# One pass of the attention scores made for two slots at once, on quarters of TensorE's rows

## The chip, the cores and the metric

The kernel runs on one core of a Trainium2 chip. The metric is the time of one execution on the device, in microseconds (us). The unchanged kernel takes 734.6 us, the median of three runs.

## The reference

A block on x of shape (2, 1024, 128): causal attention with a residual, a mixture of experts, a state space layer, and the mixture again. Only the attention is touched. Cut to what matters:

```
qk = layernorm(x) @ W_qk;  q, k = split(qk)          # 16 heads of 64, two batches of 1024 tokens
scores = einsum('bhid,bhjd->bhij', q * 64**-0.5, k)  # masked above the diagonal
out = einsum('bhij,bhjd->bhid', softmax(scores), k)  # the keys are also the values
x = x + out @ W_out
```

## The kernel before

**Units.** The attention works in 16 units: a pair of heads in one of the two batches. A head of the pair has 64 rows, so head l = 0 lies on partitions 0 to 63 and head l = 1 on partitions 64 to 127. Most products of the attention are made for both heads by two matmuls, one on each half of TensorE's rows (the profile writes such a tile 64*128, rows by columns).

**Slots.** The masked scores of a unit are laid out transposed (keys on partitions, queries along the free axis) in nine slots of 512 columns for each head, with one or two segments in a slot (`SLOTS`). Slots 0 and 3 to 7 are one segment of 512 columns, slot 1 is 384 + 128, slot 2 is 256 + 256, slot 8 is 384 + 128. `scores(unit, slot)` makes four passes over each segment, for both heads in each: high keys by high queries (L753), high by low (L756), low by high (L759), and a pass that subtracts each query's maximum (L762). In that last pass the stationary operand is all ones, and the moving operand `m_rows` holds the negated maxima: eight rows of each head's 64 are used, one for each tile of 128 queries, picked by `neg_pick`; all other rows are zero. For diagonal slots (0, 1, 2, 7, 8) `mask` adds the mask first (L738).

**The maxima** of unit u+1 are found one unit ahead: `max_scores` (ten fills "M", L716) makes plain scores on TensorE, `maxima` on VectorE (L583, L587) reduces them into `half_max`, and `join_maxima` (L596) joins the halves into `row_max`. `turn_max` transposes that (L726), and `max_rows` (L601) spreads it into `m_rows`.

**The order** is written out by hand. Each unit after the first goes through five rounds:

```
ROUNDS = [[("mask", 0), ("M", 0), ("S", 0), ("M", 1)],
          [("mask", 1), ("mask", 2), ("M", 2), ("S", 1), ("S", 2), ("M", 3)],
          [("M", 4), ("S", 3), ("S", 4), ("M", 5)], [("M", 6), ("S", 5), ("S", 6), ("M", 7)],
          [("mask", 7), ("mask", 8), ("M", 8), ("S", 7), ("S", 8), ("M", 9)]]
```

At the start of a round TensorE makes `outputs` of the previous unit (probabilities by keys, L783, tile 128*64), and in rounds 1 and 3 `denominators` (L802, tile 128*32). After round 4 it projects the keys "K" and queries "Q" of the unit after next (L680 to L682, tile 128*128). Unit 0 has an order of its own, `FIRST_ROUNDS`, in which S and M alternate. Unit 15 has no M, and units 14 and 15 project nothing.

**The ring.** Every T (transposed keys), M, S, K and Q takes the next of three pairs of PSUM banks, in strict rotation (`ring_uses`). `pair_free` makes TensorE wait until the use three places earlier has been read. So M 4 takes the banks of S 1, S 3 those of S 2, M 6 those of S 3, S 5 those of S 4, S 7 those of S 6, K those of S 7, and Q those of S 8. A slot's banks come free when ScalarE has taken its exponentials (L525, one instruction of 1024 columns for each slot, slots in order).

**Other engines.** GpSimd adds up the probabilities for the denominators (`add_up`, L427), eleven sums to a unit, the first of which needs slot 1. VectorE also makes the low parts and scales the outputs. SyncE loads weights and spreads the inverted denominators.

Of the kernel before, what the change touches and what calls it, by code (L numbers as in the profile page):

```python
# [20 lines left out]
ALU = mybir.AluOpType  # L21
# [3 lines left out]
P = 128  # L25
# [212 lines left out]
def attention(nc, k, w_qk, x_view, load_w_out):  # L238
# [5 lines left out]
    with Scope(nc, "at") as s:  # L244
# [31 lines left out]
        knat_ps_ready, knat_done = s.sem("knat_ps_ready"), s.sem("knat_done")  # L276
        max_ready, max_taken, row_max_done = s.sem("max_ready"), s.sem("max_taken"), s.sem("row_max_done")
        rows_ps_ready, rows_done = s.sem("rows_ps_ready"), s.sem("rows_done")
        scores_ready, exp_done, av_done, summed = s.sem("scores_ready"), s.sem("exp_done"), s.sem("av_done"), s.sem("summed_up")
        den_ready, ln_done, inv_done, out_used = s.sem("den_ready"), s.sem("ln_done"), s.sem("inv_done"), s.sem("out_used")  # L280
        inv_spread = [s.sem(f"inv_spread{h}") for h in range(2)]

# [2 lines left out]
        def rows(l):  # L285

            return slice(DH * l, DH * l + DH)

        def dens(g, halves):

# [51 lines left out]
        def split_w(pool, p):  # L342
            pool.wait_ge(w_loaded, 16 * (p + 1))
            wait(pool, proj_ready, 4 * (p - 1))
            pool.tensor_copy(w_hi[p % 2][:, :, :], w_raw[:, :, :]).then_inc(w_split, 1)
            pool.wait_ge(w_split, 2 * p + 1)
            pool.tensor_tensor(w_lo[p % 2][:, :, :], w_raw[:, :, :], w_hi[p % 2][:, :, :].bitcast(FP32),
                               ALU.subtract).then_inc(w_split, 1)

        def set_up(pool):  # L350
            pool.memset(k.eps[:, :], EPS).then_inc(k.ident_made, 1)
            pool.memset(k.ident[:, :], 0.0).then_inc(k.ident_made, 1)
            pool.wait_ge(k.ident_made, 2)
            pool.affine_select(out=k.ident[:, :], in_=k.ident[:, :], compare_op=ALU.not_equal, fill=1.0,
                               base=0, pattern=[[-1, P]], channel_multiplier=1).then_inc(k.ident_made, 1)
            pool.memset(eye2[:, :, :], 0.0).then_inc(consts, 1)
            pool.memset(mask2[:, :, :], 0.0).then_inc(consts, 1)
            pool.memset(neg_pick[:, :], 0.0).then_inc(consts, 1)
            pool.memset(after_query[:, :], 0.0).then_inc(consts, 1)
            pool.wait_ge(consts, 4)  # L360
            pool.affine_select(out=after_query[:, BANK - P:BANK], in_=after_query[:, BANK - P:BANK], compare_op=ALU.is_ge,
                               fill=MASKED, base=0, pattern=[[-1, P]], channel_multiplier=1).then_inc(consts, 1)
            pool.wait_ge(consts, 5)
            for l in range(2):
                pool.affine_select(out=eye2[rows(l), :, :], in_=eye2[rows(l), :, :], compare_op=ALU.not_equal, fill=1.0,
                                   base=0, pattern=[[DH, 2], [-1, P]], channel_multiplier=1).then_inc(consts, 1)
                pool.affine_select(out=mask2[rows(l), :, :], in_=mask2[rows(l), :, :], compare_op=ALU.is_ge, fill=MASKED,
                                   base=0, pattern=[[DH, 2], [-1, P]], channel_multiplier=1).then_inc(consts, 1)
                pool.affine_select(out=neg_pick[rows(l), :], in_=neg_pick[rows(l), :], compare_op=ALU.not_equal, fill=-1.0,
                                   base=0, pattern=[[-1, QT]], channel_multiplier=1).then_inc(consts, 1)  # L370
            pool.wait_ge(consts, 11)
            split_w(pool, 0)

        def clear(dve):
# [9 lines left out]
        with nc.Block() as block:  # L384
# [83 lines left out]
            def _(act):  # L468
# [49 lines left out]
                    act.activation(to, to, ACT.Exp, scale=-1.0).then_inc(inv_done, 1)  # L518

                def exponentials(unit, slot):  # L520
                    act.wait_ge(scores_ready, 2 * (NSLOT * unit + slot) + 2)
                    if unit:
                        act.wait_ge(av_done, 2 * (NBURST * (unit - 1) + BURST_OF[slot]) + 2)
                        act.wait_ge(summed, NSUM * (unit - 1) + SUMMED_AT[slot] + 1)
                    act.activation(probs[:, :, slot * BANK:(slot + 1) * BANK], pair("S", unit, slot)[:, :, :], ACT.Exp,  # L525
                                   scale=BETA).then_inc(exp_done, 1)
# [41 lines left out]
            def _(dve):  # L568
# [24 lines left out]
                def join_maxima(unit):  # L593
                    dve.wait_ge(max_taken, NMAX * (unit + 1))
                    wait(dve, rows_ps_ready, 2 * unit)
                    dve.reduce_max(row_max[:, :, 0:QT], half_max[:, :, :, :], AX.X).then_inc(row_max_done, 1)  # L596

                def max_rows(unit):

# [38 lines left out]
                for m in range(6, NMAX):  # L638
                    maxima(0, m)
                join_maxima(0)  # L640
                dve.wait_ge(consts, 11)
                for unit in range(UNITS):
                    more = unit + 1 < UNITS
                    for r, row in rounds(unit):
# [24 lines left out]
            def _(pe):  # L669
# [50 lines left out]

                def turn_max(unit):

                    pe.wait_ge(row_max_done, unit + 1)
                    wait(pe, ln_done, 2 * unit - 1)
                    for l in range(2):
                        pe.matmul(misc[rows(l), 0:P], row_max[:, l, :], k.ident[:, :], start=True, stop=True)\  # L726
                          .then_inc(rows_ps_ready, 1)
# [13 lines left out]
                def scores(unit, slot):  # L741

                    u, out, first = unit % 2, pair("S", unit, slot), slot not in DIAGONAL
                    if slot == 0:
                        pe.wait_ge(rows_done, unit + 1)
                        pe.wait_ge(k_low, unit + 1)
                        pe.wait_ge(q_low, unit + 1)
                    pair_free(pe, "S", unit, slot)
                    for seg, (j, a, b) in enumerate(SLOTS[slot]):
                        q, keys, o = slice(a * P, b * P), slice(j * P, (j + 1) * P), at_slot(slot, seg) - slot * BANK  # L750
                        to = [out[:, l, o:o + (b - a) * P] for l in range(2)]
                        for l in range(2):
                            pe.matmul(to[l], kh[u][rows(l), keys], qh[u][rows(l), q], start=first, stop=False,  # L753
                                      skip_group_check=True)
                        for l in range(2):
                            pe.matmul(to[l], kh[u][rows(l), keys], ql[u][rows(l), q], start=False, stop=False,  # L756
                                      skip_group_check=True)
                        for l in range(2):
                            pe.matmul(to[l], kl[u][rows(l), keys], qh[u][rows(l), q], start=False, stop=False,  # L759
                                      skip_group_check=True)  # L760
                        for l in range(2):
                            last = pe.matmul(to[l], ones_r[rows(l), :], m_rows[u][rows(l), q], start=False, stop=True,  # L762
                                             skip_group_check=True)
                            if seg + 1 == len(SLOTS[slot]):
                                last.then_inc(scores_ready, 1)

                def outputs(g, r):

# [67 lines left out]
                turn_keys(1)  # L836
                turn_max(0)
                warm(5, out_ps)
                pe.wait_ge(consts, 11)

                for unit in range(UNITS + 1):
                    more = unit + 1 < UNITS
                    for r, row in rounds(unit):
                        if r == 0 and 0 < unit < UNITS:
                            turn_max(unit)
                        if unit:
                            outputs(unit - 1, r)
                        if r == (1 if unit < UNITS else 3) and unit:
                            denominators(unit - 1, 1)
                        if unit == UNITS:  # L850
                            continue
                        if r == (3 if unit else 4):
                            denominators(unit, 0)
                        if r == 0 and unit and more:
                            turn_keys(unit + 1)
                        for what, n in row:
                            if what == "mask":
                                mask(unit, n)
                            elif what == "S":
                                if n in DIAGONAL and not unit:  # L860
                                    mask(unit, n)
                                scores(unit, n)
                            elif more:
                                max_scores(unit + 1, n)
                        if r == NBURST - 1 and unit + 2 < UNITS:
                            project(unit + 2, "K")
                            project(unit + 2, "Q")
# [1023 lines left out]
```

## Time and profile before

| | |
|---|---|
| median of 3 runs | 734.6 us (734.4 to 735.08) |
| the profiled execution | 734.34 us |
| its span in the profile | 732.5 us |
| TensorE busy | 706.9 us (96%) |
| VectorE, ScalarE, GpSimd busy | 434.5, 371.4, 417.4 us |
| granted TensorE clock over the span | 0.993 |

The attention fills the stretch up to about 452 us, the rest is the two mixtures and the state space layer. In the profile PE is TensorE's matmuls, PEld its weight loads, DVE VectorE, ACT ScalarE, POOL GpSimd. Matmul records overlap, since the array is pipelined: what a pass costs is the distance from its start to the next start, not the duration printed beside it.

### The profile page before, as it was taken

How to read it: one execution, taken by the hardware profiler on the slowest of the kernel's cores; microseconds unless marked ns; L12 is line 12 of the kernel's file. 1: busy time of each engine (PE TensorE's matmuls, PEld its weight loads, DVE VectorE, ACT ScalarE, POOL GpSimd, SP SyncE). 2: the span in 40 equal slices, each digit the busy share in tenths (PEclk: the TensorE clock that was granted, in tenths of full speed). 3: DMA queues.
4: the chain of work that ended last, by engine and by line, in shares of the span. 5: the costliest groups of instructions: out<-in, count | busy, mean ns of one | idle time of the engine just before them, and what ended most of it. 6: DMA issues, size and time to landing. Idle time of an engine off the chain costs nothing. (4 is left out here: it accounts for less than half of the span.)

```text
span 732.5 us, 14992 instructions
## 1 busy us (share of the span) xinstructions
PE 706.9 (96%) x5681; PEld 498.8 (68%) x5681; DVE 434.5 (59%) x1214; ACT 371.4 (51%) x478; POOL 417.4 (57%) x310
## 2 busy tenths in 40 slices
PE   7999999999999999999999899999999999889998
PEld 5665666566665566566656555978888865678887
DVE  7776765765676676676567600635654656755433
ACT  4465655555555555465555442364664343566421
POOL 4486677668559659658756864144544421254543
PEclk9799999999999999999999999999999999999999
DMA  2001001001001100100100112623323000043332
GB/s 72 8 17 26 24 19 30 24 16 30 24 18 28 30 16 22 36 17 17 30 16 16 30 44 63 153 89 103 98 79 102 1 0 1 12 134 103 105 103 72
DMA packets 41276, 33.49 MB, mean 46 GB/s; under 512 B 14002, under 2 KB 32756, under 8 KB 41204
## 3 DMA queue, kind: packets, MB, share of 16 engines
q1 hardware_dynamic: 41204, 32.52, 15.5%
q8 instruction: 46, 0.75, 0.4%
q14 instruction: 26, 0.21, 0.1%
HBM read 23.32 MB, written 1.31 MB: 34 GB/s over the span
## 5 line engine op out<-in xcount | busy, mean ns | idle before, releaser
L427 POOL TENSOR_TENSOR all_x<-all_x,at_probs 128x1024 f32<-128x1024 f32 (+3 forms) x128 | 208.2, 1627 | 19.0 <-ACT at_probs L525 0.4
L525 ACT ACTIVATE at_probs<-at_ring 128x1024 f32<-128x1024 f32 x144 | 144.3, 1026 | 100.6 <-PE at_ring L762 99.4
L587 DVE CUSTOM_DVE_ANT_0 at_ring<-at_ring,at_after_query 128x128 f32<-128x128 f32 (+3 forms) x252 | 116.9, 516 | 68.9 <-PE at_ring L716 68.9
L783 PE MATMUL at_both<-at_probs,at_k_nat 128*64 128x512 f32 (+1 forms) x736 | 134.3, 493 | 0.2 <-issue 0.2
L1279 POOL TENSOR_TENSOR m_prod<-m_gate,m_wb 128x512 f32<-128x512 f32 x64 | 81.5, 1281 | 91.0 <-ACT m_gate L1141 81.8
L427 POOL TENSOR_TENSOR all_x<-at_probs 128x768 f32<-128x768 f32 (+1 forms) x32 | 67.3, 2104 | 106.6 <-ACT at_probs L525 103.9
L583 DVE TENSOR_REDUCE at_half_max<-at_ring 128x2 f32<-128x1024 f32 x64 | 78.4, 1226 | 44.9 <-PE at_ring L716 44.9
L783 PEld LDWEIGHTS at_both<-at_probs,at_k_nat 128*64 128x64 f32 x736 | 47.0, 136 | 65.3 <-issue 54.3
L1195 DVE TENSOR_TENSOR m_hid<-m_prod,m_u 128x512 f32<-128x512 f32 x64 | 43.6, 686 | 75.7 <-POOL m_prod L1279 69.3
L1057 PEld LDWEIGHTS m_acc<-rest_wd,m_hid 128*128 128x128 f32 (+1 forms) x576 | 74.4, 191 | 7.9 <-DVE m_hid L1195 2.2
L1057 PE MATMUL m_acc<-rest_wd,m_hid 128*128 128x128 f32 (+1 forms) x576 | 76.1, 276 | 0.0
L1141 ACT ACTIVATE m_gate<-m_g 128x512 f32<-128x512 f32 (+1 forms) x72 | 42.6, 597 | 64.2 <-PE m_g L1048 63.0
L716 PE MATMUL at_ring<-at_kh,at_qh 64*128 64x512 f32 (+2 forms) x380 | 70.8, 396 | 1.0 <-ACT a_room L478 0.5
L759 PE MATMUL at_ring<-at_qh,at_kl 64*128 64x512 f32 (+3 forms) x384 | 67.1, 343 | 0.0
L753 PE MATMUL at_ring<-at_qh,at_kh 64*128 64x512 f32 (+3 forms) x384 | 67.0, 344 | 0.1
L762 PE MATMUL at_ring<-at_m_rows,at_ones_r 64*128 64x512 f32 (+3 forms) x384 | 66.9, 342 | 0.0
L756 PE MATMUL at_ring<-at_ql,at_kh 64*128 64x512 f32 (+3 forms) x384 | 66.8, 342 | 0.0
L716 PEld LDWEIGHTS at_ring<-at_kh,at_qh 64*128 64x128 f32 x380 | 34.6, 187 | 27.0 <-issue 25.5
L753 PEld LDWEIGHTS at_ring<-at_qh,at_kh 64*128 64x128 f32 x384 | 36.7, 185 | 4.6 <-ACT at_probs L525 0.8
L759 PEld LDWEIGHTS at_ring<-at_qh,at_kl 64*128 64x128 f32 x384 | 36.6, 185 | 4.0
L762 PEld LDWEIGHTS at_ring<-at_m_rows,at_ones_r 64*128 64x128 f32 x384 | 36.7, 185 | 3.8
L756 PEld LDWEIGHTS at_ring<-at_ql,at_kh 64*128 64x128 f32 x384 | 36.5, 185 | 3.8
(256 smaller groups left out, 1194.6 us busy)
## 6 DMA issues: line engine op xcount, KB each, us to landing
m_wb<-m_wt_far SPq DMA_DIRECT2D x128, 128.0 KB, 2.9
at_inv<-at_inv_q SPq DMA_DIRECT2D x240, 32.0 KB, 1.9
all_x<-in_L_attn_a_x SPq DMA_DIRECT2D x8, 256.0 KB, 4.2
at_w_raw<-in_L_attn_a_W_qk SPq DMA_DIRECT2D x8, 128.0 KB, 2.6
out<-all_x SPq DMA_DIRECT2D x4, 256.0 KB, 2.3
a_room<-in_L_attn_a_W_out SPq DMA_DIRECT2D x1, 512.0 KB, 4.1
m_raw_wg<-in_L_ffn_experts_wg SPq DMA_DIRECT2D x1, 512.0 KB, 3.8
m_raw_wu<-in_L_ffn_experts_wu SPq DMA_DIRECT2D x1, 512.0 KB, 3.9
```

Source lines behind the costliest of these rows:

```text
L427: return pool.tensor_tensor(sums[:, :, a * P:b * P], left, right, ALU.add)
L525: act.activation(probs[:, :, slot * BANK:(slot + 1) * BANK], pair("S", unit, slot)[:, :, :], ACT.Exp, scale=BETA).then_inc(exp_done, 1)
L583: last = dve.reduce_max(half_max[:, :, i, out], pair("M", unit, m)[:, :, at:at + w], AX.X)
L587: last = dve.tensor_tensor_reduce(out=sums_ps, in0=sums_ps, in1=after_query[:, BANK - w:BANK], scale=1.0, scalar=MASKED, op0=ALU.add, op1= ...
L716: last = pe.matmul(out[:, l, at:at + (b - a) * P], qh[u][rows(l), i * P:(i + 1) * P], kh[u][rows(l), a * P:b * P], start=True, stop=True)
L753: pe.matmul(to[l], kh[u][rows(l), keys], qh[u][rows(l), q], start=first, stop=False, skip_group_check=True)
L756: pe.matmul(to[l], kh[u][rows(l), keys], ql[u][rows(l), q], start=False, stop=False, skip_group_check=True)
L759: pe.matmul(to[l], kl[u][rows(l), keys], qh[u][rows(l), q], start=False, stop=False, skip_group_check=True)
L762: last = pe.matmul(to[l], ones_r[rows(l), :], m_rows[u][rows(l), q], start=False, stop=True, skip_group_check=True)
L783: last = pe.matmul(out_bank(g, int(r > 0))[rows(l), o:o + (b - a) * P], k_nat[g % 3][:, j, rows(l)], probs[:, l, at:at + (b - a) * P], sta ...
L1057: last = pe.matmul(acc[:, t * P:(t + 1) * P], hid[g % BUFS][h, t * P:(t + 1) * P], f.wd[h, st, :], start=(st == 0 and t == 0), stop=(st == ...
L1279: pool.tensor_tensor(prod[g % BUFS][:, :], gate[g % BUFS][:, :], wb[q % SPREAD][:, :], ALU.mult)\
```

## The change

The last of the four passes is taken out of `scores` and put into a function of its own, `shift(unit, slots)`. In units 1 to 15 it is called once in a round, behind the last S of the round, for all slots of the round (one in round 0, two in rounds 1 to 4). In unit 0 it is called behind each slot. It uses 32 rows for a matmul in place of 64: the first slot of a call takes rows 0 to 31 (head 0) and 64 to 95 (head 1), the second rows 32 to 63 and 96 to 127. For that, `join_maxima` writes the maxima twice, 32 columns apart, and `neg_pick` gets its diagonal twice, by two more instructions of GpSimd in the set-up. ScalarE now waits on one of two semaphores, for even and for odd slots. `turn_max` waits for both reductions.

```
+        def quarter_rows(l, n):
+            return slice(DH * l + DH // 2 * n, DH * l + DH // 2 * (n + 1))
...
             pool.wait_ge(consts, 11)
+            for l in range(2):
+                pool.affine_select(out=neg_pick[rows(l), :], in_=neg_pick[rows(l), :], compare_op=ALU.not_equal, fill=-1.0,
+                                   base=-DH // 2, pattern=[[-1, QT]], channel_multiplier=1).then_inc(consts, 1)
+            pool.wait_ge(consts, 13)
             split_w(pool, 0)
...
                 def exponentials(unit, slot):
-                    act.wait_ge(scores_ready, 2 * (NSLOT * unit + slot) + 2)
+                    of = (NSLOT + 1 - slot % 2) // 2
+                    act.wait_ge(shifted[slot % 2], 2 * (of * unit + slot // 2) + 2)
...
                     dve.reduce_max(row_max[:, :, 0:QT], half_max[:, :, :, :], AX.X).then_inc(row_max_done, 1)
+                    dve.reduce_max(row_max[:, :, DH // 2:DH // 2 + QT], half_max[:, :, :, :], AX.X).then_inc(row_max_done, 1)
...
-                    pe.wait_ge(row_max_done, unit + 1)
+                    pe.wait_ge(row_max_done, 2 * unit + 2)
...
-                        for l in range(2):
-                            last = pe.matmul(to[l], ones_r[rows(l), :], m_rows[u][rows(l), q], start=False, stop=True,
-                                             skip_group_check=True)
-                            if seg + 1 == len(SLOTS[slot]):
-                                last.then_inc(scores_ready, 1)
+
+                def shift(unit, slots):
+                    u = unit % 2
+                    for seg in range(2):
+                        for n, slot in enumerate(slots):
+                            if seg >= len(SLOTS[slot]):
+                                continue
+                            j, a, b = SLOTS[slot][seg]
+                            o = at_slot(slot, seg) - slot * BANK
+                            for l in range(2):
+                                r = quarter_rows(l, n)
+                                last = pe.matmul(pair("S", unit, slot)[:, l, o:o + (b - a) * P], ones_r[r, :],
+                                                 m_rows[u][r, a * P:b * P], start=False, stop=True, skip_group_check=True)
+                                if seg + 1 == len(SLOTS[slot]):
+                                    last.then_inc(shifted[slot % 2], 1)
...
                                 scores(unit, n)
+                                if not unit:
+                                    shift(unit, [n])
+                                elif n == slots[-1]:
+                                    shift(unit, slots)
```

## Rows read from the trace of the kernel before

**Rows 1.** The page's busy time: us, share of the span, instructions.

```profile
PE 706.9 (96%) x5681; PEld 498.8 (68%) x5681; DVE 434.5 (59%) x1214; ACT 371.4 (51%) x478; POOL 417.4 (57%) x310
```

**Rows 2.** Windows: unit 11, from one L726 to the next; stretch, length, busy us.

```profile
315.18:341.58 26.40, 26.40 (x250) 16.66 (x249) 17.53 (x42) 14.56 (x19) 17.61 (x11) 1.00 0.09 22
```

**Rows 3.** Timeline of PE, rounds 1 to 3 of unit 11: start, us, instruction, operands.

```profile
322.88 0.34 PE L753 MATMUL at_ring<-at_qh,at_kh 64*128 64x384 f32 x2
...
324.86 0.28 PE L762 MATMUL at_ring<-at_m_rows,at_ones_r 64*128 64x256 f32 x2
324.98 0.34 PE L716 MATMUL at_ring<-at_kh,at_qh 64*128 64x384 f32 x2
325.24 1.08 PE L783 MATMUL at_both<-at_probs,at_k_nat 128*64 128x512 f32 x4
326.25 0.50 PE L716 MATMUL at_ring<-at_kh,at_qh 64*128 64x512 f32 x2
326.59 0.40 PE L753 MATMUL at_ring<-at_qh,at_kh 64*128 64x512 f32 x2
...
333.68 1.94 PE L783 MATMUL at_both<-at_probs,at_k_nat 128*64 128x512 f32 x12
```

**Rows 4.** Timeline of PE, round 4 of unit 11, slots 7 and 8, and K.

```profile
336.19 0.39 PE L753 MATMUL at_ring<-at_qh,at_kh 64*128 64x512 f32 x2
...
336.88 0.40 PE L762 MATMUL at_ring<-at_m_rows,at_ones_r 64*128 64x512 f32 x2
337.12 0.34 PE L753 MATMUL at_ring<-at_qh,at_kh 64*128 64x384 f32 x2
...
337.64 0.34 PE L762 MATMUL at_ring<-at_m_rows,at_ones_r 64*128 64x384 f32 x2
337.81 0.22 PE L753 MATMUL at_ring<-at_qh,at_kh 64*128 64x128 f32 x2
...
338.10 0.27 PE L762 MATMUL at_ring<-at_m_rows,at_ones_r 64*128 64x128 f32 x2
338.21 0.44 PE L716 MATMUL at_ring<-at_kh,at_qh 64*128 64x512 f32 x2
338.58 0.50 PE L680 MATMUL at_ring<-all_xhi,at_w_hi 128*128 128x512 f32 x1
338.92 0.39 PE L681 MATMUL at_ring<-all_xlo,at_w_hi 128*128 128x512 f32 x1
```

**Rows 5.** Timeline of ACT: exponentials of slots 7, 8 (unit 10) and 1, 2 (unit 11).

```profile
310.95 2.12 ACT L525 ACTIVATE at_probs<-at_ring 128x1024 f32<-128x1024 f32 x2 [2.73 <-PE at_ring L762]
...
324.21 2.02 ACT L525 ACTIVATE at_probs<-at_ring 128x1024 f32<-128x1024 f32 x2 [1.03 <-PE at_ring L762]
```

**Rows 6.** Timeline of POOL and PE, unit 11: the sums, then the denominators.

```profile
327.81 2.16 POOL L427 TENSOR_TENSOR all_x<-all_x,at_probs 128x256 f32<-128x256 f32 x2
...
330.60 0.64 PE L802 MATMUL at_both<-all_x,at_ones 128*32 128x256 f32 x8
```

**Rows 7.** Timeline: the end of POOL's set-up, and DVE's joining.

```profile
4.80 0.20 POOL L369 TENSOR_SCALAR_AFFINE_SELECT at_neg_pick<-at_neg_pick 64x8 f32<-64x8 f32 x1
6.11 0.40 POOL L345 CAST at_w_hi<-at_w_raw 128x256 fp32r<-128x256 f32 x1 [1.11 <-DMA at_w_raw<-in_L_attn_a_W_qk]
...
313.76 0.19 DVE L596 TENSOR_REDUCE at_row_max<-at_half_max 128x16 f32<-128x32 f32 x1
```

**Rows 8.** Timeline of ACT and PE, ends of units 0 and 14.

```profile
47.17 1.02 ACT L525 ACTIVATE at_probs<-at_ring 128x1024 f32<-128x1024 f32 x1 [0.60 <-PE at_ring L762]
...
48.34 0.47 PE L680 MATMUL at_ring<-all_xhi,at_w_hi 128*128 128x512 f32 x1 [0.69 <-ACT at_probs L525]
...
419.58 0.44 PE L726 MATMUL at_both<-all_ident,at_row_max 128*64 128x128 f32 x4 [1.75 <-DVE at_row_max L596]
```

**Rows 9.** Timeline of POOL and PE, last unit: first sum, last denominators.

```profile
428.69 1.82 POOL L427 TENSOR_TENSOR all_x<-at_probs 128x768 f32<-128x768 f32 x1 [5.20 <-ACT at_probs L525]
...
447.73 1.08 PE L797 MATMUL at_both<-all_x,at_ones 128*64 128x512 f32 x4 [0.63 <-POOL all_x L427]
```

More of the change, by code:

```diff
@@ L278, in attention @@
         rows_ps_ready, rows_done = s.sem("rows_ps_ready"), s.sem("rows_done")
-        scores_ready, exp_done, av_done, summed = s.sem("scores_ready"), s.sem("exp_done"), s.sem("av_done"), s.sem("summed_up")
+        shifted = [s.sem("shifted_even"), s.sem("shifted_odd")]
+        exp_done, av_done, summed = s.sem("exp_done"), s.sem("av_done"), s.sem("summed_up")
         den_ready, ln_done, inv_done, out_used = s.sem("den_ready"), s.sem("ln_done"), s.sem("inv_done"), s.sem("out_used")
@@ L640, in _ @@
                 join_maxima(0)
-                dve.wait_ge(consts, 11)
+                dve.wait_ge(consts, 13)
                 for unit in range(UNITS):
@@ L838, in _ @@
                 warm(5, out_ps)
-                pe.wait_ge(consts, 11)
+                pe.wait_ge(consts, 13)
                 for unit in range(UNITS + 1):
@@ L855, in _ @@
                             turn_keys(unit + 1)
+                        slots = [n for what, n in row if what == "S"]
                         for what, n in row:
```

## The prediction

> **What bounds the kernel now.** I read the page first: TensorE is busy for 96% of the span, no other engine over 60% [rows 1]. A share says little, so next the windows of single units. From one L726 to the next a unit takes 26.40 us with PE busy for all 26.40, while ACT has 14.56, DVE 17.53 and POOL 17.61 [rows 2]. So for units 1 to 13 each us that TensorE saves or spends inside a unit shows in the end, unless something then makes it wait. Third the timeline of TensorE inside that unit. The reader is to look at distances between starts. A pass of 512 columns for both heads moves the next start by 0.24 (336.88 to 337.12), one of 384 by 0.17, one of 128 by 0.11 [rows 4], one of 256 by 0.12 [rows 3]. Last ACT's timeline, since a slot's banks are held until its exponential is done [rows 5]. ACT is idle half of the time, but what counts is when its work ends against the ring.
>
> **The saving.** L762's passes now cost, in round 1 (slots 1 and 2), 0.17 + 0.11 + 0.12 + 0.12 = 0.52 us; in rounds 2 and 3 two passes of 512, 0.46; in round 4, 0.24 + 0.17 + 0.11 = 0.52 [rows 3, 4]. With two slots side by side the wider segment of each pair counts: round 1 0.17 + 0.12 = 0.29, rounds 2 and 3 0.23 each, round 4 0.24 + 0.11 = 0.35. Saved: 0.23 + 0.23 + 0.23 + 0.17 = 0.86 us a unit. Round 0 has one slot and saves nothing. That four tiles run together I take from the denominators: eight matmuls of 256 columns on quarters of the columns take 0.64 us in all [rows 6], far below eight in a row. No row has quarters of the rows.
>
> On four tiles of 32 rows the Trainium skill (TensorE: Matmul & The Clock Gate, "Measured speedup vs the span model") gives a measured speed-up of 3.07 for 512 columns, not 4. By that, as an estimate, a pass of four would take 0.24 x 4 / 3.07 = 0.31 in place of 0.24, and the sum below would be some 3 us higher; no row here shows it.
>
> **The switches.** The trace does not show a change from tiles of 64 rows to tiles of 32. It shows every other change of tile, and none is free. From 64*128 to 128*128: the pass of 512 columns at 338.21 is followed after 0.37, not 0.24, and the first one in the new tile after 0.34 (338.58 to 338.92) [rows 4]; so 0.13 before and 0.10 after. From 64*128 to 128*64 a pass of 384 takes 0.26 in place of 0.17, 0.09 more; back at 64*128 the first pass of 512 takes 0.34, 0.10 to 0.11 more [rows 3]. I read these as the array running empty, and then a weight load with nothing to hide behind. One switch is thus 0.20 to 0.24 us. The `shift` passes lie between scores and M, both on 64*128, so each round gets two more switches, 0.41 us with the lower figures. Bounds: 0 below (if a change among divisions of rows is not a change at all), 0.46 above. I take 0.41, since all kinds that are shown pay, among them the one in which only the number of rows differs.
>
> The Trainium skill (TensorEngine Tiling (Array Packing), "Key Properties") states that changing the tiling mode, not just the tile, drains the engine, and counts 64 and 32 rows as different modes. The rows agree for every change that they hold. By that rule rounds 0 to 4 spend 2.05 us on switches to save 0.86; without it the saving stands alone.
>
> **The exponentials come later.** Before, ACT could begin on the first slot of a round while TensorE made the second. Now both slots are ready at the end, and two exponentials of 1.02 stand in a row behind them [rows 5]. Two uses of the ring stand close behind.
>
> *Round 1, S 3 waits for slot 2's banks.* Before: exponentials from 324.21 to 326.23 [rows 5], S 3 at 326.59 [rows 3], 0.36 to spare. Now: slots 1 and 2 start at 322.88 and M 3 follows at 324.98; less 0.52 the three other passes end at 324.46. Running empty 0.09 and load 0.11: 324.66. The second pass of four starts 0.17 later and lands 0.28 after its start: 325.11. ACT follows 0.07 later (slot 7's pass 336.88 + 0.40 = 337.28, its exponential one unit of 26.40 before at 310.95 [rows 4, 5]): 325.18. Two exponentials, 2.02: 327.20. From ACT's end to TensorE's start 0.15 (47.17 + 1.02 = 48.19 to 48.34 [rows 8]): S 3 at 327.35, against 326.59 + 0.18 by TensorE's own work (0.41 - 0.23). So a wait of 0.58, and round 1 costs 0.76.
>
> *Round 4, K waits for slot 7's banks.* Before: K at 338.58 [rows 4], slot 7's exponential done some 0.2 earlier. Now: the other passes end at 338.21 - 0.52 = 337.69, + 0.20 switch + 0.40 for the pass + 0.07 + 1.02 + 0.15 = K at 339.53. That is 0.95 late, of which TensorE's own work is 0.41 - 0.17 = 0.24 and 0.71 is a wait. Behind K in TensorE's queue stand Q, the next unit's L726 and outputs, all late by the same; ACT's and DVE's copies of K and Q follow K as before. Q needs slot 8, done about 1 us after slot 7, when K's 1.4 us of passes are still running: no wait.
>
> *Rounds 2 and 3.* The same lateness meets 1.94 us of outputs before the next use [rows 3]: no wait with the switches, 0.41 - 0.23 = +0.18 each. *Round 0*: +0.41, no wait.
>
> Sum for a unit of 1 to 13: 0.41 + 0.76 + 0.18 + 0.18 + 0.95 = 2.48 us, times 13 = 32.2 us.
>
> **The other units.** Unit 0 has nine calls with one slot each: nothing saved, nine times 0.41 = 3.7. It has waits that take some up, but its K stands behind slot 8's exponential already [rows 8], so most goes through: 3.4, bounds 0 and 9 x 0.46 = 4.1. Unit 14 projects nothing and ends on DVE (1.75 us of idle TensorE before L726 [rows 8]): what counts is when M 9 starts, 337.69 + 0.20 + 0.24 + 0.11 + 0.09 = 338.33, 0.12 late in round 4. 0.41 + 0.76 + 0.18 + 0.18 + 0.12 = 1.65, plus the second joining, 0.19 at most [rows 7]: 1.8. Unit 15 ends on GpSimd: its sums run almost without a gap from 428.69 until the last denominators, which wait 0.63 for them [rows 9], and the first of them needs slot 1. Slot 1's exponential comes 0.97 late as in round 1, plus 0.2 from round 0's switch (no M follows there, so one switch more, not two): 1.2.
>
> **What I cost at nothing.** The two instructions in GpSimd's set-up, 0.20 each [rows 7], lie under a wait of 1.11 us for weights; without it, 0.4. The second joining in units 1 to 13 lies under K and Q: the first begins at 313.76 [rows 7] and L726, which waits for it, at 315.18 [rows 2], 1.2 after its end. In unit 0 it does not: 0.2. Queued behind it on DVE is the scaling of outputs, which nobody waits for at once. The sums on GpSimd start 0.97 later; the two that the denominators need end at 329.97, now 330.94, while TensorE comes to them at 330.60 + 0.76 + 0.18 = 331.54 [rows 6]. No DMA changes.
>
> Sum: 32.2 + 3.4 + 1.8 + 1.2 + 0.2 = 38.8 us. The profiled execution took 734.34 (span 732.5), 0.26 below the median. 734.3 + 38.8 = 773.1; I forecast 772. With 0.46 for two switches all rounds but the waits' share grow by 0.05 each, some 3 us; with 0 it is rival A.
>
> **The rivals.**
>
> *A, free switches, late exponentials.* For it: no row has this change of tile. Against: all others pay. Round 0 gives 0. Round 1: 324.46 + 0.17 + 0.28 + 0.07 + 2.02 + 0.15 = 327.15, +0.56. Round 2 -0.23. Round 3 -0.13, as S 7's mask would now wait 0.1 for slot 6. Round 4: 337.69 + 0.40 + 0.07 + 1.02 + 0.15 = 339.33, +0.75. 0.95 x 13 = 12.4, units 14 and 15 1.0, joining 0.2: 748. The mode rule above is what stands against it. Switches that cost half lie between, at 760.
>
> *B, the quarters do not run side by side*, so the change does not do what it says: slots' passes one behind the other. The 0.86 are not saved in 14 units, and the last landing is later still by up to 0.2: 772 + 12 = 784. Against: a pair on two halves of the rows takes 0.24, hardly more than one matmul of 512 columns would alone at 2.4 GHz, and quarters of columns overlap [rows 4, 6].
>
> *C, faster.* Its place is the ring: if the exponentials' lateness were hidden at S 3 and at K, and the switches free, 0.86 x 14 = 12 us come off: 722. It decides where slot 2 is done before TensorE gets to S 3, that is 0.8 us earlier than my sum has it. Against: ACT needs 2.02 for the pair, and between the shift and S 3 stand only M 3, 1.0 of outputs and M 4 [rows 3]. I see no way round.
>
> **How the numbers follow.** Full switches: 62%, its own range 763 (waits a third shorter than worked out) to 780 (the upper bound of the switches and of unit 0, and passes of four slower than pairs). A and half-price switches: 23%, 746 to 762. B: 8%, 781 to 790. C: 5%. No change (waits and saving cancel): 2%. The range takes in the first two and stops at 746 and 781, which leaves out C, most of B and no change. Within 0.2% (1.5 us) is what a measurement can't tell from no change: faster 0.05, same 0.02, slower 0.93.
>
> **What would show it.** In the changed kernel L762's successor should stand in tiles 32*128, with a gap of 0.1 before it and 0.34 for its first pass of 512. A unit should take 28.9 us. TensorE should be idle twice a unit: before L753 of slot 3 (0.6) and before L680 (0.7), both put down to L525. ACT's pairs should start 1 us later in the round. Were the passes 0.24 apart with no gap, A is right; four starts in two steps of 0.23 would be B. The prediction is wrong above all if the switch within divisions of rows costs other than 0.2.

## The result, and the profile after

The changed kernel takes 767.4 us (median of 4 runs, 767.0 to 767.66) against 734.64 for the kernel before: a ratio of 1.0446, 95% interval 1.0434 to 1.0458. It is slower by 32.8 us. The forecast was 772, within 746 to 781. The four executions spread by 0.66 us, so the noise doesn't matter to the sign or the size.

The page of the changed kernel: its span and the busy time of the engines.

```profile
span 765.4 us, 15012 instructions
...
PE 724.0 (95%) x5681; PEld 488.9 (64%) x5681; DVE 436.3 (57%) x1230; ACT 368.3 (48%) x478; POOL 417.0 (54%) x312
```

TensorE is busy for 17 us more than in [rows 1], with the same number of matmuls, and for 16 us more it is not busy. Both halves of the prediction are in these two numbers, but which is which the page can't say: a matmul whose weights are still being loaded counts as busy. So, windows of one unit, the changed kernel's unit 11, as in [rows 2]:

```profile
337.96:366.42 28.46, 27.42 (x250) 15.96 (x249) 17.69 (x43) 14.32 (x19) 17.32 (x12) 1.00 0.08 20
```

28.46 us in place of 26.40, of which TensorE is busy 27.42. Units 1 to 13 have 28.41 to 28.52. Now the same unit's timeline of PE, round 0 and then rounds 1 and 2; it answers to [rows 3].

```profile
341.94 0.42 PE L770 MATMUL at_ring<-at_qh,at_kl 64*128 64x512 f32 x2
342.30 0.50 PE L784 MATMUL at_ring<-at_m_rows,at_ones_r 32*128 32x512 f32 x2
342.73 0.50 PE L727 MATMUL at_ring<-at_kh,at_qh 64*128 64x512 f32 x2
343.16 1.51 PE L805 MATMUL at_both<-at_probs,at_k_nat 128*64 128x512 f32 x8
...
347.37 0.28 PE L770 MATMUL at_ring<-at_qh,at_kl 64*128 64x256 f32 x2
347.58 0.51 PE L784 MATMUL at_ring<-at_m_rows,at_ones_r 32*128 32x384 f32 x8
348.02 0.44 PE L727 MATMUL at_ring<-at_kh,at_qh 64*128 64x384 f32 x2
348.39 1.08 PE L805 MATMUL at_both<-at_probs,at_k_nat 128*64 128x512 f32 x4
349.40 0.51 PE L727 MATMUL at_ring<-at_kh,at_qh 64*128 64x512 f32 x2
350.14 0.50 PE L764 MATMUL at_ring<-at_qh,at_kh 64*128 64x512 f32 x2 [0.23 <-ACT at_probs L535]
...
351.40 0.39 PE L770 MATMUL at_ring<-at_qh,at_kl 64*128 64x512 f32 x2
351.72 0.50 PE L784 MATMUL at_ring<-at_m_rows,at_ones_r 32*128 32x512 f32 x4
352.15 0.44 PE L727 MATMUL at_ring<-at_kh,at_qh 64*128 64x384 f32 x2
352.52 1.94 PE L805 MATMUL at_both<-at_probs,at_k_nat 128*64 128x512 f32 x8
```

Read round 2 first, where nothing waits. The last score pass of 512 columns is followed after 0.32, not 0.23 (351.40 to 351.72): 0.09 for running empty. The four subtracting matmuls are followed after 0.43 (to 352.15): a pass of 0.23, an exposed weight load of 0.11, and 0.09 of running empty again. M 5, 384 columns, takes 0.37 where M 3 of the same width takes 0.26 in [rows 3]: another exposed load. So the trip to quarters and back costs 0.09 + 0.11 + 0.09 + 0.11 = 0.40, and saves 0.23. In round 1 slot 3's first pass starts 0.74 behind M 4 (349.40 to 350.14) where 0.34 is the usual distance: a wait of 0.40, of which the row shows 0.23 as idle; the rest lies under M 4's printed length.

The rows hold one thing more. The eight subtracting matmuls of round 1 (384 and 256 columns, then 128 and 256) are followed after 0.44 (347.58 to 348.02), and so are the six of round 4 (512 and 384, then 128: 361.72 to 362.16, below), as against 0.43 for the four of 512. In all three a quarter of the rows gets 512 columns in all. Two segments behind one another cost no more than one wide one.

Round 4, PE and ACT of the changed kernel, answering to [rows 4, 5]:

```profile
361.52 0.27 PE L770 MATMUL at_ring<-at_qh,at_kl 64*128 64x128 f32 x2
361.72 0.51 PE L784 MATMUL at_ring<-at_m_rows,at_ones_r 32*128 32x512 f32 x6
362.16 0.50 PE L727 MATMUL at_ring<-at_kh,at_qh 64*128 64x512 f32 x2
363.46 0.47 PE L691 MATMUL at_ring<-all_xhi,at_w_hi 128*128 128x512 f32 x1 [0.81 <-ACT at_probs L535]
```
```profile
348.14 1.94 ACT L535 ACTIVATE at_probs<-at_ring 128x1024 f32<-128x1024 f32 x2 [1.93 <-PE at_ring L784]
...
362.29 1.94 ACT L535 ACTIVATE at_probs<-at_ring 128x1024 f32<-128x1024 f32 x2 [3.02 <-PE at_ring L784]
```

K starts 0.15 after the first exponential of the pair (362.29 + 1.02 = 363.31), with TensorE idle for 0.81. Counted from the unit's L726 (before) or L737 (after), the starts are as follows; the last column gives what each round adds:

| start of | before | after | late by | in the round |
|---|---|---|---|---|
| outputs, round 1 | 4.94 | 5.20 | 0.26 | 0: 0.26 |
| S 3 | 11.41 | 12.18 | 0.77 | 1: 0.51 |
| S 5 | 16.32 | 17.34 | 1.02 | 2: 0.25 |
| S 7 | 21.01 | 22.18 | 1.17 | 3: 0.15 |
| K | 23.40 | 25.50 | 2.10 | 4: 0.93 |

### The profile page after: what moved, and what is told of

Same layout as the page of the kernel before. It is cut to its first block and busy times, and to the rows that moved or that the text cites. A ratio compares the mean times of both kernels' runs of the same rounds, so it can differ in the third digit from the quotient of the medians.

```text
span 765.4 us, 15012 instructions
## 1 busy us (share of the span) xinstructions
PE 724.0 (95%) x5681; PEld 488.9 (64%) x5681; DVE 436.3 (57%) x1230; ACT 368.3 (48%) x478; POOL 417.0 (54%) x312
## 5 line engine op out<-in xcount | busy, mean ns | idle before, releaser
L535 ACT ACTIVATE at_probs<-at_ring 128x1024 f32<-128x1024 f32 x144 | 141.0, 1022 | 145.0 <-PE at_ring L784 145.0
L727 PE MATMUL at_ring<-at_kh,at_qh 64*128 64x512 f32 (+2 forms) x380 | 76.6, 428 | 1.2 <-ACT a_room L487 0.5
L727 PEld LDWEIGHTS at_ring<-at_kh,at_qh 64*128 64x128 f32 x380 | 33.7, 186 | 36.5 <-issue 32.2
L784 PE MATMUL at_ring<-at_m_rows,at_ones_r 32*128 32x512 f32 (+3 forms) x384 | 42.3, 411 | 0.0
L691 PE MATMUL at_ring<-all_xhi,at_w_hi 128*128 128x512 f32 x60 | 25.2, 421 | 12.0 <-ACT at_probs L535 11.0
```

The lines of the kernel that those rows point to most:

```text
L727: last = pe.matmul(out[:, l, at:at + (b - a) * P], qh[u][rows(l), i * P:(i + 1) * P], kh[u][rows(l), a * P:b * P], start=True, stop=True)
```

## The experiments

All figures for a unit are of unit 11, and lengths are from one L726 (or its successor) to the next. Each kernel has one profiled execution, and all windows and lines are of that one. The unchanged kernel had medians of 734.3 to 734.69 beside them.

**1. Late, but on halves.** It asks what the lateness alone costs.

```
-                                r = quarter_rows(l, n)
+                                r = rows(l)
```

and one copy of the maxima, as before.

> The subtracting passes stay at the end of the round, but on halves of the rows, slot after slot: no second tiling, nothing saved, one copy of the maxima. My theory (late exponentials and switches both cost): slot 3's start waits, 324.46 + the passes up to slot 1's last start 0.40, + 0.17 + 0.27 more to land and be seen, ACT's pair 1.94, 0.06: some 0.5 us late; K 337.69 + 0.40 + 0.07 + 1.02 + 0.15 = 339.33, 0.75 late. 1.25 a unit times 13, 0.5 in unit 14, 0.9 in unit 15: 734.6 + 17.7 = 752. Rival (only the switches cost, the waits would vanish without them): 735. Rival (only the lateness costs): near the changed kernel, 765.

Measured 753.81 us, ratio 1.0266 (1.0249 to 1.0283), close to the 752 expected. A unit takes 27.70, 1.30 more, 0.45 of it before S 3 and 0.77 in round 4. The waits of PE in the unit (us in total, times, longest):

```profile
PE at_ring L686 <- ACT at_probs L531: 0.7, 1, 0.7
PE at_ring L759 <- ACT at_probs L531: 0.3, 1, 0.3
```

The same two places wait without any change of tiling, so the rival that ties the waits to the switches falls. But it makes 19.5 of the 33 us (1.0 of them before unit 0 begins, at 32.25 and not 31.26), so lateness is not all.

**2. Late, on one quarter for both slots.** It asks whether the four matmuls really run together.

```
-                                r = quarter_rows(l, n)
+                                r = quarter_rows(l, 0)
```

> As the changed kernel, but both slots of a call use the first quarter of each head's rows, so they cannot run side by side. My theory: the saving of four tiles at once is real, so 0.2 comes back in each of rounds 1 to 3 and nothing in round 4, where slot 7's pass goes first either way and K waits for its exponential: 0.6 times 13, 0.8 in unit 14: 767.4 + 8.6 = 776. Rival (the quarters don't overlap in the changed kernel either): 767.

Measured 776.16, ratio 1.0563 (1.0545 to 1.0581), and 776 was expected. A unit takes 29.07. Round 2's passes:

```profile
358.05 0.73 PE L784 MATMUL at_ring<-at_m_rows,at_ones_r 32*128 32x512 f32 x4
358.71 0.44 PE L727 MATMUL at_ring<-at_kh,at_qh 64*128 64x384 f32 x2
```

0.66 from the first to M 5 where the changed kernel has 0.43: the second slot's pass costs its full 0.23 here and nothing there. The overlap is real, and worth 29.07 - 28.46 = 0.61 a unit, not 0.86. By the starts of S 3, S 5, S 7 and K in the two kernels, rounds 1 to 4 give 0.12, 0.25, 0.23 and 0.01: the wait for the exponentials swallows part of it in round 1 and all of it in round 4.

Experiments 1 and 2 and the changed kernel make a ladder, in us a unit: 26.40, + 1.30 for lateness = 27.70, + 1.37 for the switches = 29.07, - 0.61 for the overlap = 28.46. The 1.37 are less than five times 0.35 to 0.40, since part of the trips passes under the two waits.

**3. Quarters behind each slot.** It asks what the switches alone cost.

```
-                                if not unit:
-                                    shift(unit, [n])
-                                elif n == slots[-1]:
-                                    shift(unit, slots)
+                                shift(unit, [n])
```

> The passes on quarters, but each behind its own slot as in the kernel before: nothing is late, nothing saved, nine trips to the other tiling and back in a unit. My theory: 0.26 in round 0 and 0.38 for each of eight others, 3.3 us a unit times 13, 3.3 in unit 14, 2.6 in unit 15, 2.4 in unit 0: 734.6 + 51 = 786, TensorE without the two waits on ACT. Rival (lateness is all): 735 to 740.

Measured 783.27, ratio 1.0665 (1.0647 to 1.0683), 3 us under my figure of 786. The rival (lateness is all) had 735 to 740. The unit's window has no idle TensorE:

```profile
350.07:379.60 29.53, 29.53 (x250) 16.55 (x249) 17.70 (x43) 14.78 (x19) 17.59 (x12) 1.00 0.07 19
```

3.13 more than 26.40 for nine trips. One of them, 512 columns for one slot between score passes:

```profile
362.83 0.40 PE L770 MATMUL at_ring<-at_qh,at_kl 64*128 64x512 f32 x2
363.16 0.50 PE L784 MATMUL at_ring<-at_m_rows,at_ones_r 32*128 32x512 f32 x2
363.59 0.50 PE L764 MATMUL at_ring<-at_qh,at_kh 64*128 64x512 f32 x2
363.93 0.40 PE L767 MATMUL at_ring<-at_ql,at_kh 64*128 64x512 f32 x2
```

Three distances, 0.33 + 0.43 + 0.34 = 1.10, where three passes of 0.23 would be 0.69: 0.41 for the trip, as forecast from other kinds of tile. It is the change that costs, not the tile: in experiment 2 a second pass on 32 rows, with no change before it, costs 0.23 like one on 64. Trips next to passes of 128 to 384 columns cost less, which makes the mean 0.35.

**4. Round 4 put back.** In the changed kernel, round 4 makes its passes on halves behind each slot again, with a second tile of ones whose rows under the second copy of the maxima are zero.

```
+                                elif r == NBURST - 1:
+                                    shift(unit, [n], halves=True)
```

> As the changed kernel, but round 4 has its passes on halves behind each slot again (with a second tile of ones whose rows under the second copy are zero). My theory: round 4 gives back its 0.93 in 13 units: 767.4 - 12.3 = 755, and TensorE's wait before the keys' projection is gone. Rival (the cost is TensorE's own work, the wait is slack): 0.24 times 13 come back, 764.

Measured 757.22, ratio 1.0313 (1.0296 to 1.033). A unit takes 27.53 to 27.58, 0.91 less than the changed kernel's on the mean. Of the waits of PE in units 1 to 13 the one before K is gone, and the one before S 3 is left. The changed kernel (first) and this one, from 55 to 415 us:

```profile
PE at_ring L691 <- ACT at_probs L535: 9.6, 12, 0.8
PE at_ring L764 <- ACT at_probs L535: 3.1, 13, 0.2
```
```profile
PE at_ring L768 <- ACT at_probs L539: 3.1, 13, 0.2
```

So the rival that called the wait slack (764) falls. My sum gave TensorE's own work 0.24 of the round. The rows give it some 0.06: in the changed kernel as in the one before, M 9 starts 2.02 behind slot 7's first pass (360.14 to 362.16; 336.19 to 338.21 in [rows 4]), and only its weight load is then open (in experiment 3, where K waits for nothing, M 9 takes 0.42 to K and not 0.37). Nearly all of the 0.93 is the wait. The time came out 2 us above my figure of 755: unit 0 begins at 32.45 and not 31.00, and unit 15 takes 1.65 us longer than the changed kernel's (taken up under experiment 5), while the stretch behind the attention takes 1.3 less.

**5. Pairs in rounds 2 and 3 only**, all other passes on halves behind their slots as in the kernel before. The second copy of the maxima and experiment 4's second tile of ones stay.

```
+                                if not unit or r not in (2, 3):
+                                    shift(unit, [n], halves=True)
+                                elif n == slots[-1]:
+                                    shift(unit, slots)
```

> Pairs of slots on quarters only in rounds 2 and 3, where 1.94 us of outputs stand before the next use of the banks; all other rounds and unit 0 as before, on halves behind each slot. My theory: no waits, two trips of 0.39 less two savings of 0.23: 0.32 to 0.36 a unit times 14, and 0.2 for the second joining in unit 0: 734.6 + 5 = 739.6. Rival (without the waits the saving wins): 734.6 - 15 x 0.46 = 728.

Measured 741.32, ratio 1.0089 (1.0075 to 1.0102), 1.7 above the 739.6 expected and far from the rival's 728. A unit takes 26.70 (26.69 to 26.73 over the units), 0.3 more: two trips less two savings, with no wait. Even where nothing is late, the pair loses. The 13 units make 4 us of the 6.5 in its span. Another 1.8 are in unit 15, where nothing was forecast. Windows of this kernel and, second, of the changed one at the start of unit 15, right behind a wait of 1.84 us of TensorE for the operand of L726 (now L741 and L737), which VectorE makes; the last three columns are the granted clock, the DMA share and GB/s:

```profile
424.00:429.00 5.00, 4.52 (x26) 2.25 (x26) 2.01 (x4) 0.00 (x0) 4.17 (x3) 0.66 0.00 0
```
```profile
449.90:454.90 5.00, 4.80 (x36) 2.52 (x38) 2.40 (x3) 0.54 (x1) 3.84 (x3) 1.00 0.00 0
```

Behind the same wait the clock stays at 1.00 in the changed kernel; here it averages 0.66 over 5 us, that is, it is at 1.2 GHz for part of them. The first sixteen matmuls of the outputs take 3.99 us here and 2.38 there. Experiment 4 has the same in its unit 15 (0.74 in one window of 5 us), and so have the profiled executions of experiments 2 and 3 (0.66 each, from 459 to 464 and from 468 to 473 us).

**6. One pair, behind the last M of round 2**, so that only one more switch is made.

```
+                                if not unit or r != 2:
+                                    shift(unit, [n], halves=True)
...
+                        if unit and r == 2:
+                            shift(unit, slots)
```

> One pair only, round 2's, and its passes stand behind the round's last M, next to the change of tiling that is there anyway: one more switch, not two. My theory: 0.20 - 0.23 = -0.03 a unit, the exponentials 0.3 later still, done 0.6 before slot 5 needs the banks; with the second joining in unit 0: 734.6 - 0.4 + 0.2, 734.4, no difference. Rival (a switch next to a switch is free): 15 x 0.23 off, 731.3. Rival (the later exponentials are waited for): over 737.

Measured 740.38, ratio 1.0073 (1.0059 to 1.0086): my figure of 734.4 was wrong. A unit takes 26.69, 0.29 more, not 0.03 less. PE and DVE in round 2:

```profile
331.02 0.40 PE L774 MATMUL at_ring<-at_qh,at_kl 64*128 64x512 f32 x2
331.46 0.44 PE L731 MATMUL at_ring<-at_kh,at_qh 64*128 64x384 f32 x2
331.83 0.51 PE L788 MATMUL at_ring<-at_m_rows,at_ones_r 32*128 32x512 f32 x4
332.27 0.65 PE L809 MATMUL at_both<-at_probs,at_k_nat 128*64 128x512 f32 x2
```
```profile
330.09 1.23 DVE L597 TENSOR_REDUCE at_half_max<-at_ring 128x2 f32<-128x1024 f32 x1 [0.30 <-PE at_ring L731]
```

M 5 comes 0.44 behind the pass before it, not 0.23. It takes the banks of M 4, which VectorE reads until 330.09 + 1.23 = 331.32. With two passes less ahead of it M 5 is ready too early and waits 0.2 for VectorE, then shows its weight load of 0.1 (0.37 to the next start in place of 0.26). I had checked the ring's uses by ScalarE, and not those by VectorE. The switch itself is right, 0.44 from 331.83 to 332.27, less the pass of 0.23: 0.21. So the sum is 0.21 for the wait, 0.11 for the load, 0.21 for the switch, less 0.23: 0.30, of 0.29 measured. The rival that had a switch next to a switch free (731.3) is wrong, and so is the one that had the exponentials waited for (over 737), though its time fits: the pair ends at 332.40 + 1.94 = 334.34, and S 5, which takes slot 4's banks, starts at 335.05. The 13 units make 4.0 us of the 6.3 in the span; another 1.6 are behind the attention, where the clock of the profiled execution fell (0.83 from 640 to 650 us).

**7. The maxima in bf16**, in the kernel before; it asks for a cheaper pass without another tiling.

```
-        ones_r = s.sb("ones_r", [P, P], F32R)
+        ones_r = s.sb("ones_r", [P, P], BF16)
```

and `m_rows` likewise.

> The kernel before, with the rows of the maxima and their tile of ones in bf16 in place of fp32r; one subtracted value a query serves all its keys and its denominator, so its rounding cancels. It asks whether the pass can be made cheaper without another tiling. The load of ones should take about half (the masks' bf16 load has 95 ns against 185), so a pass of 128 columns costs 0.06 in place of 0.11, twice a unit, while passes of 256 to 512 cover their loads anyway: 0.1 a unit, 734.6 - 1.6 = 733. Rival (a bf16 matmul among fp32r ones has a price of its own, as a change of tiling has): 736 or more.

Measured 734.59 against 734.54, ratio 0.9995 (0.9985 to 1.0005): no difference. Its unit of 26.29 is 0.10 shorter, as forecast, 1.3 us in 13 units; but in the profile unit 15 is 1.6 us longer, with this behind the wait for VectorE:

```profile
418.00:423.00 5.00, 4.58 (x26) 2.24 (x26) 1.95 (x3) 0.00 (x0) 3.88 (x3) 0.66 0.00 0
```

A gain of 0.1 a unit is of the size of what the clock gives or takes behind one wait. The executions bear that out: at a mean granted clock of 0.995 this kernel has one, 732.22 us, and the kernel before beside it has five, 733.94 to 734.15. But most of its executions (eight of eleven) have 0.991. None of the seven kernels is shown to beat the one before.

## Why the prediction was right, step by step

**The bound.** Right. TensorE set the units' length before, and what was added showed in full, 13 times.

**The saving.** The four tiles run together: four matmuls of 512 columns take the 0.43 that two take in experiment 3 (351.72 to 352.15, 363.16 to 363.59). The slower passes of four that the Trainium skill's speed-up of 3.07 gives (TensorE: Matmul & The Clock Gate, "Measured speedup vs the span model") would have stretched this by 0.07; by these rows they did not, and the measurement decides. In rounds 1 and 4 the passes saved more than my sum had: I let the wider segment of each pair count, 0.29 and 0.35, where the rows have 0.44 less 0.20 for load and running empty, 0.24 each. Little of it reached the time: experiment 2 gives the overlap 0.61 a unit, nothing of it in round 4, which my sum had at 0.95 whatever TensorE saves.

**The switches.** The term that carried most of the doubt, 0.41 for two, came out at 0.40 to 0.41 between passes of 512 (round 2 after; experiment 3) and at a mean of 0.35. The rule of the Trainium skill (TensorEngine Tiling (Array Packing), "Key Properties") that a change of mode drains the engine holds for 64 to 32 rows, 0.09 a time; the page has no price, and the rows show as much again, 0.11, for the weight load that then lies open. Rival A (748) and half-price switches (760) fall with it, and rival B (784) with experiment 2. The number alone would not have done that: the range of 746 to 781 took in free and half-price switches as well.

**Round 0** was mis-sized, 0.41 against 0.26. M 1 takes the banks of T, and in the kernel before its start was behind ScalarE's copy of T already. ACT and PE before, unit 11:

```profile
318.46 1.09 ACT L502 ACTIVATE at_k_nat<-at_ring 128x512 f32<-128x512 f32 x2 [1.72 <-PE at_ring L701]
```
```profile
319.41 0.41 PE L762 MATMUL at_ring<-at_m_rows,at_ones_r 64*128 64x512 f32 x2
319.69 0.50 PE L716 MATMUL at_ring<-at_kh,at_qh 64*128 64x512 f32 x2
320.12 0.65 PE L783 MATMUL at_both<-at_probs,at_k_nat 128*64 128x512 f32 x2
```

The copy ends at 319.55 and M 1 starts at 319.69, 0.28 behind the pass before it. It takes 0.43 to the outputs, and takes 0.43 after. An open load was there to begin with, so the switch back did not add one.

**Round 1**, 0.76 against 0.51. The exponentials began 0.08 before my figure (348.14, 10.18 after L737, against 10.00 by the step and 0.26 from round 0), the pair took 1.94 instead of 2.02, and S 3 started 0.06 behind their end, not 0.15: a wait of 0.40, not 0.58. TensorE's own work grew by 0.11, not 0.18, as the eight passes took 0.44 and not 0.49. The 0.15 was taken from K's start at another place, and K keeps it (363.31 to 363.46); why S 3 follows faster is open. The step's mechanism was right, its wait 0.18 too long.

**Rounds 2 and 3**, 0.18 each against 0.25 and 0.15. Round 2 has 0.10 that my sum lacked: behind its wait S 3's first pass shows its load, 0.34 to the next start (350.14 to 350.48) in place of 0.24. **Round 4**, 0.95 against 0.93: the chain to K was right, with K 0.15 behind the exponential and TensorE idle for 0.81 (0.71 forecast). The split was not: 0.06 of TensorE's own work, not 0.24, and a longer wait in its place. Experiment 4 shows the wait as the cause.

**The other units.** Units 1 to 13 cost 2.07 each (2.48 forecast), 26.9 in all, not 32.2. Unit 0 took 22.42 in place of 20.04, 2.4 (3.4 forecast), also since its trips cost less than 0.41. Unit 14 took 1.3 more (1.8 forecast), unit 15 up to the next stage 33.4 in place of 32.1, 1.3 (1.2 forecast). The set-up cost nothing, and the second joining nothing in units 1 to 13. Ahead of unit 0 TensorE waits 0.56 for it where it waited 0.47, and at the start of unit 15 1.84 where it waited 1.75: 0.1 each.

**What I did not have.** From the end of attention on, where the two kernels have the same instructions, the changed one took 1.3 us more. It is in one place at the start of the second mixture, behind a wait of TensorE for VectorE of 1.79 us that both have. Windows of after and, second, of before, in about the same work:

```profile
668.00:672.00 4.00, 4.00 (x25) 3.87 (x24) 1.37 (x4) 0.75 (x2) 1.27 (x1) 0.68 0.06 12
```
```profile
636.00:640.00 4.00, 3.96 (x30) 3.56 (x30) 2.26 (x7) 1.67 (x3) 1.27 (x1) 1.00 0.05 12
```

The sum is 26.9 + 2.4 + 1.3 + 1.3 + 1.3 - 0.3 (a somewhat faster start) = 32.9, the difference of the spans. So the 772 was some 6 us high in units 0 to 13 and had nothing for this 1.3. That the two partly cancel is luck. The two large steps, the switches and the waits, had the right mechanism. What was too large are round 0's switch back, the wait before S 3 and the price of the trips next to narrow passes.

## What to carry to other kernels

Packing small matmuls into more tiles of the array has to save more than the trip to the other tiling costs, unless the work around them is in that tiling already: here a trip out and back costs 0.4 us, nearly two passes of 512 columns, and a pair saves one. Work that is put off so that it can be shared makes its readers late as well: before moving it, list the next uses of each buffer it fills, by every engine that reads it, with the time to spare (0.36 and 0.2 us here, against exponentials that come 1.0 later). And a use that comes earlier wants the same look: in experiment 6 a matmul that moved up met a reader that had not been late for anyone.

## What the runs showed of the hardware

- A change between tiles of 64 and of 32 rows costs as much as one between 64 and 128: 0.09 us before the first pass and 0.11 in it.
- Four matmuls on four quarters of the rows, into four banks, take no longer than two (0.43 from first start to the next work, both ways). Six and eight narrower ones with the same 512 columns a quarter take 0.44.
- Behind a wait of 1.8 us on TensorE the clock can fall to 1.2 GHz, and need not. All nine kernels have two such waits. In their profiled executions it fell behind the one at the start of unit 15 in experiments 2, 3, 4, 5 and 7, for 1.6 to 1.8 us of lost time, and behind the one in the second mixture in the changed kernel and in experiments 2, 3 and 6, for 1.3 to 1.7 us. What decides it these runs do not show, and it need not be the kernel: the unchanged one, beside experiments 5 and 6, took 734.19 to 735.06 us in seven executions, at mean granted clocks of 0.993 to 0.995, and 736.57 to 736.61 in three, at 0.990 and 0.991. So a difference of 1 to 2 us between two kernels is read from units at a granted clock of 1.00, not from one execution's time.
